# Two attention blocks on one core: residual copies replaced by additions that read x and x1 themselves

## The chip, the cores and the metric

The kernel runs on one core of a Trainium2 chip. A core has TensorE (PE, matrix products into PSUM; PEld is its weight load), VectorE (DVE), ScalarE (ACT), GpSimd (POOL) and SyncE (SP, which here issues every DMA). The engines run on their own and meet only at semaphores. The metric is the device time of one execution in microseconds, the median of several runs. Lower is better.

## The reference

Eight images of 256 channels and 32 x 32 pixels pass two attention blocks in a row, all in float32:

```
x : (8, 256, 1024)                       # image, channel, pixel
# layer 0
q = Wq x + bq ; k = Wk x + bk            # 32 channels each
v = Wv x + bv                            # 256 channels
x1 = gamma * (v softmax(q^T k)^T) + x
# layer 1
h  = group_norm(x1, 32 groups of 8 channels) * norm_w + norm_b
q, k, v = 256-channel projections of h, with biases
y  = x1 + proj( v softmax(q^T k / 16)^T ) + proj_b
```

Each layer therefore ends in a residual: layer 0 adds x, layer 1 adds x1. Since the rows of a softmax sum to one, the bias bv of layer 0 comes out as the constant gamma*bv per channel, and the output bias proj_b is a constant per channel too.

## The kernel before, in words

An image lies in SBUF as 128 partitions x 2 channel tiles (`CT`) x 1024 pixels. Products are made in near-float32 accuracy from pairs of a high and a low part (`_hi`, `_lo`), three matmuls for each product (`three`, lines 553 to 556). So every tensor that enters a product is split: mostly ACT writes the high part and DVE the low part.

The order of the work is written out by hand as a list of `Step`s (lines 78 to 199), and PE, ACT and DVE each walk through the same list. In the steady part one image takes a turn of 16 steps (`turn(i)`): the first 8 steps make the layer 0 attention tiles of image i (`keys`), the last 8 make the layer 1 attention tiles of image i - 1 (`logits`). The values product of a tile (`values`) follows its probabilities by two steps. So the layer 1 output of image i - 2 is complete in step 1 of turn i, and the layer 0 output of image i in step 9. PSUM is a ring of four slots of 128 x 1024: slots 0 and 1 mostly hold score tiles and projections, slots 2 and 3 hold the four banks of the running values product (`pv_ps`).

What the change touches:

- `evacuate` on DVE (lines 1050 to 1061) takes the four finished banks out of PSUM, 128 x 512 each. For layer 0 it writes x1 = gamma * bank + x1, in place (line 1057), for layer 1 res1 = bank + res1, in place (line 1060). What it adds was put into those buffers beforehand.
- That is done on POOL: `residual0` (line 461) writes x1 = 1 * x + gamma*bv from `x_in`, and `residual1` (line 453) writes res1 = 1 * x1 + proj_b. `unit` is a column of ones. POOL handles these in the order coefficients of the group norm, `hidden` (h in float32, line 439), `residual1`, `residual0` of the next image, four low parts of the layer 1 values (`split_value1`, line 468).
- SP issues the loads of x (line 390) and the stores of y (line 395) in one fixed row: after the store of image i comes the load of image i + 4. A load waits until `residual0` has copied the old content of its buffer, counted by `res0_ready`.
- `statistics` on DVE (lines 1063 to 1070) takes mean and variance of x1 per channel with two bn_stats for each half and two bn_aggr. PE averages them over the groups (`group_sums`, line 643, first the means, then variance plus squared distance of means), and `norm` on DVE (lines 1037 to 1048) makes what POOL needs for scale and offset.
- After step 1's evacuation, DVE goes on in its own order to low parts of the probabilities (`pt_lo`, line 1024), the low part of h (`h_lo`, line 919) and the second half of q and k of the next image (lines 977, 978, 985). PE needs these for the first `scores` tile of image i + 1 (line 564).

`link` makes DVE wait for its own preceding instruction, by a semaphore.

## Time and profile before

| | |
|---|---|
| median of 3 runs | 804.33 us (803.9 to 804.9) |
| the profiled execution's own time | 804.08 us |
| its span in the trace | 802.3 us |
| PE busy | 783.3 us (98%) |
| PEld busy | 646.1 us (81%) |
| DVE busy | 550.9 us (69%) |
| ACT busy | 469.2 us (58%) |
| POOL busy | 161.0 us (20%) |
| bytes read and written in HBM | 9.97 MB and 8.39 MB, 23 GB/s over the span |

The granted clock of TensorE was 0.995 of full speed over the span. The profiled execution's time lies 1.8 us above its span. The engines' busy times overlap, so none of them adds to the time by itself: what counts is where PE stands still and for whom.

### The profile page before, as it was taken

The numbers are of one execution on the slowest core, as the hardware profiler recorded it, in microseconds if no ns is written. First come the engines' busy times: TensorE is split into PE (matmuls) and PEld (weight loads), VectorE is DVE, ScalarE is ACT, GpSimd is POOL, SyncE is SP. The second block draws the span as 40 slices with busy tenths as digits, with TensorE's granted clock in tenths as the row PEclk, the third lists the DMA queues.
The fourth block names the chain that finished last, engine by engine and source line by source line (L and its number), as shares of the span: only waits on it lengthen the run. The fifth ranks groups of instructions, "written<-read, shape, count | busy, mean of one in ns | idle before, by whom it ended". The sixth has DMA issues, their size and how long they took to land.

```text
span 802.3 us, 9810 instructions
## 1 busy us (share of the span) xinstructions
PE 783.3 (98%) x3816; PEld 646.1 (81%) x3816; DVE 550.9 (69%) x790; ACT 469.2 (58%) x605; POOL 161.0 (20%) x144
## 2 busy tenths in 40 slices
PE   8899989999999999999999999999999999999998
PEld 8687868887888878888788877888788888887886
DVE  5866858778578765787657785676856765575564
ACT  4886556568455775567655586456855565444342
POOL 4800142023100241004210141102310024103300
PEclk9999999999999999999999999999999999999999
DMA  6100010002000110001100011000100010000101
GB/s 184 52 1 1 1 52 1 1 2 105 1 1 1 48 58 1 1 1 53 54 1 1 1 52 53 2 1 0 53 1 1 0 46 8 1 0 1 53 1 52
DMA packets 10365, 18.98 MB, mean 24 GB/s; under 512 B 2128, under 2 KB 3920, under 8 KB 10320
## 3 DMA queue, kind: packets, MB, share of 16 engines
q1 hardware_dynamic: 10320, 18.36, 6.6%
q8 instruction: 30, 0.49, 0.3%
q14 instruction: 15, 0.12, 0.0%
HBM read 9.97 MB, written 8.39 MB: 23 GB/s over the span
## 4 chain that ended last, share of the span: by engine, by line
PE 82%; DVE 11%; ACT 5%; issue 2%; ACTq 0%; POOL 0%; DVEq 0%; POOLq 0%
PE ring L554 25%; PE ring L556 24%; PE ring L555 24%; PE ring L564 4%; PE ring L574 3%; DVE h_lo L919 2%; DVE pt_lo L1024 2%; DVE res L1060 2%; DVE q L985 1%; PE ring L551 1%; ACT prob L773 1%; ACT prob L776 1%; DVE neg_raw L1009 1%; DVE k L977 1%; ACT pt_hi L787 1%
## 5 line engine op out<-in xcount | busy, mean ns | idle before, releaser
L554 PE MATMUL ring<-pt_hi,v_hi 128*128 128x512 f32 x512 | 202.8, 396 | 0.6 <-DVE pt_lo L1027 0.6
L556 PE MATMUL ring<-pt_hi,v_lo 128*128 128x512 f32 x512 | 201.2, 393 | 0.0
L555 PE MATMUL ring<-pt_lo,v_hi 128*128 128x512 f32 x512 | 201.1, 393 | 0.0
L776 ACT ACTIVATE prob<-ring,neg_max 128x1024 f32<-128x1024 f32 x64 | 71.6, 1118 | 160.2 <-DVE neg_max L1010 160.2
L468 POOL TENSOR_TENSOR v_lo<-v_f,v_hi 128x512 fp32r<-128x512 f32 x32 | 43.2, 1351 | 424.7 <-ACT v_hi L814 424.7
L1009 DVE TENSOR_REDUCE neg_raw<-ring 128x1 f32<-128x1024 f32 x64 | 78.3, 1223 | 71.6 <-PE ring L556 71.5
L554 PEld LDWEIGHTS ring<-pt_hi,v_hi 128*128 128x128 f32 x512 | 96.7, 189 | 21.8 <-issue 1.6
L556 PEld LDWEIGHTS ring<-pt_hi,v_lo 128*128 128x128 f32 x512 | 96.6, 189 | 21.3
L555 PEld LDWEIGHTS ring<-pt_lo,v_hi 128*128 128x128 f32 x512 | 96.9, 189 | 19.0
L1024 DVE TENSOR_TENSOR pt_lo<-prob,pt_hi 128x1024 fp32r<-128x1024 f32 x64 | 80.5, 1258 | 35.7 <-ACT pt_hi L787 35.5
L1007 DVE TENSOR_REDUCE neg_max<-ring 128x1 f32<-128x1024 f32 x64 | 77.8, 1222 | 33.7 <-PE ring L564 33.5
L554 PE MATMUL ring<-h_hi,query_hi 128*128 128x512 f32 x256 | 100.4, 392 | 0.0
L555 PE MATMUL ring<-h_lo,query_hi 128*128 128x512 f32 x256 | 99.9, 390 | 0.0
L556 PE MATMUL ring<-h_hi,query_lo 128*128 128x512 f32 x256 | 99.9, 390 | 0.0
L797 ACT ACTIVATE ring<-ring,neg_max 128x1024 f32<-128x1024 f32 x64 | 69.5, 1085 | 45.4 <-DVE neg_max L1007 45.0
L1027 DVE SCALAR_TENSOR_TENSOR pt_lo<-prob,row_inv,pt_hi 128x1024 fp32r<-128x1024 f32 x64 | 83.7, 1307 | 12.0 <-ACT pt_hi L790 12.0
L773 ACT ACTIVATE prob<-ring 128x1024 f32<-128x1024 f32 x64 | 65.4, 1021 | 33.6 <-PE ring L574 33.5
L790 ACT ACTIVATE pt_hi<-prob,row_inv 128x1024 fp32r<-128x1024 f32 x64 | 73.7, 1152 | 9.7 <-DVE row_inv L1016 9.6
L787 ACT CAST pt_hi<-prob 128x1024 fp32r<-128x1024 f32 x64 | 67.3, 1051 | 5.3
L556 PEld LDWEIGHTS ring<-h_hi,query_lo 128*128 128x128 f32 x256 | 48.1, 188 | 10.2
L554 PEld LDWEIGHTS ring<-h_hi,query_hi 128*128 128x128 f32 x256 | 48.1, 188 | 10.0 <-DVE v_lo L965 0.2
L555 PEld LDWEIGHTS ring<-h_lo,query_hi 128*128 128x128 f32 x256 | 48.1, 188 | 9.6
(135 smaller groups left out, 1225.5 us busy)
## 6 DMA issues: line engine op xcount, KB each, us to landing
out_y<-res SPq DMA_DIRECT2D x32, 256.0 KB, 2.2
x_in<-in_x SPq DMA_DIRECT2D x7, 1024.0 KB, 4.8
x_in<-in_x SPq DMA_DIRECT2D x2, 512.0 KB, 5.0
h_f<-in_wv_t SPq DMA_DIRECT2D x1, 256.0 KB, 4.4
res<-in_wq SPq DMA_DIRECT2D x1, 256.0 KB, 7.1
res<-in_wk SPq DMA_DIRECT2D x1, 256.0 KB, 7.3
res<-in_wv SPq DMA_DIRECT2D x1, 256.0 KB, 7.6
res<-in_wp_t SPq DMA_DIRECT2D x1, 256.0 KB, 7.7
```

Of the source, the lines that this page charges most:

```text
L554: mm(out, w_hi, m_hi, start=first, stop=False)
L555: mm(out, w_hi, m_lo, start=False, stop=False)
L556: return mm(out, w_lo, m_hi, start=False, stop=last)
L773: activation(prob[:, p % PROBS], ring[:, slot], ACT.Exp).then_inc(S["keys_exp"], 1)
L776: activation(prob[:, p % PROBS], ring[:, slot], ACT.Exp, bias=neg_max[:, k % 2:k % 2 + 1], accum_out=row_sum[:, k % 2:k % 2 + 1]).then_inc ...
L787: copy(pt_hi[p % PT][:], prob[:, p % PROBS]).then_inc(S["p_hi"], 1)
L790: activation(pt_hi[p % PT][:], prob[:, p % PROBS], ACT.Identity, scale=row_inv[:, k % 2:k % 2 + 1]).then_inc(S["p_hi"], 1)
L797: activation(ring[:, slot], ring[:, slot], ACT.Exp, bias=neg_max0[:, k:k + 1], accum_out=row_sum0[:, k:k + 1]).then_inc(S["scores_exp"], 1)
L1007: V.tensor_reduce(neg_max0[:, k:k + 1], src, AX_X, ALU.max, negate=True).then_inc(S["scores_max"], 1)
L1009: link(V.tensor_reduce(neg_raw[:, k % 2:k % 2 + 1], src, AX_X, ALU.max, negate=True))
L1024: V.tensor_tensor(lo[:], src, hi[:].bitcast(F32), ALU.subtract).then_inc(S["p_split"], 1)
L1027: V.scalar_tensor_tensor(lo[:], src, row_inv[:, k % 2:k % 2 + 1], hi[:].bitcast(F32), ALU.mult, ALU.subtract).then_inc(S["p_split"], 1)
```

## The change

`residual0` and `residual1` are gone from POOL, with `unit` and `res1`. There are now two buffers x1, used in turn by even and odd images, in the room of x1 and res1. The layer 0 evacuation reads x from `x_in` and writes gamma * bank + x to x1, so what stands there now is smaller than the true x1 by gamma*bv in each channel. The layer 1 evacuation adds its bank, x1 and a column `gbv_bp` = gamma*bv + proj_b in one instruction, in place in x1, and the stores of y read x1. The group norm is corrected by the same constant: one DVE instruction more after the two bn_aggr adds gamma*bv to the channel means, and the mean that goes into the offset of h has it subtracted (this takes the place of a copy).

The four layer 1 weight matrices, which were loaded into res1 at the start, are loaded into x1[1] now. For image 0 POOL copies x once into x1[0] (`keep_first_x`), so that image 2 can be loaded early. Every later load waits until the layer 0 evacuation has read its buffer (`pv_read`), and a layer 0 evacuation from image 2 on waits for the stores of two images before.

```diff
--- before.py
+++ after.py
...
@@ -274,11 +274,10 @@
 
         x_in = [sb(f"x_in{j}", [P, CT, N]) for j in range(2)]
         x_hi, x_lo = pair("x", [P, CT, N])
-        x1 = sb("x1", [P, CT, N])
+        x1 = [sb(f"x1_{j}", [P, CT, N]) for j in range(2)]
         h_f = sb("h_f", [P, CT, N])
         v1_f = sb("v1_f", [P, 2, 2, C])
         h_hi, h_lo = pair("h", [P, CT, N])
-        res1 = sb("res1", [P, CT, N])
         query_hi, query_lo = pair("query", [P, CT, N])
         v0_hi, v0_lo = pair("v0", [P, TILES, C])
         v1_hi, v1_lo = pair("v1", [P, TILES, C])
...
@@ -386,13 +384,16 @@
                     sp.dma_start(dst, src).then_inc(S[ready], 16)
 
             def load(i):
-                sp.wait_ge(S["res0_ready"], i - 1)
+                if i == 2:
+                    sp.wait_ge(S["x0_kept"], 1)
+                else:
+                    sp.wait_ge(S["pv_read"], PHASE_NO[0, i - 2] * BANKS + BANKS)
                 sp.dma_start(x_in[i % 2][:], x_v[i]).then_inc(x_loaded[i % 2], 16)
 
             def store(i):
                 for b, (half, ct) in enumerate(bank_of):
                     sp.wait_ge(S["pv_read"], PHASE_NO[1, i] * BANKS + b + 1)
-                    sp.dma_start(y_v[i][:, ct, half_cols[half]], res1[:, ct, half_cols[half]]).then_inc(S["y_stored"], 16)
+                    sp.dma_start(y_v[i][:, ct, half_cols[half]], x1[i % 2][:, ct, half_cols[half]]).then_inc(S["y_stored"], 16)
 
             sp.wait_ge(S["x_split"], 2)
             load(2)
...
@@ -445,22 +446,15 @@
                 pool.wait_ge(S["h_hi"], CT * i + 1)
                 G.tensor_tensor(h_lo[:, 0], h_f[:, 0], h_hi[:, 0].bitcast(F32), ALU.subtract).then_inc(S["h_split"], 1)
 
-            def residual1(i):
-                pool.wait_ge(S["bias_read"], 1)
-                if i > 0:
-                    pool.wait_ge(S["y_stored"], 16 * BANKS * i)
-                for ct in range(CT):
-                    last = G.tensor_scalar(res1[:, ct], x1[:, ct], unit[:], bp_s[:, ct:ct + 1], ALU.mult, ALU.add)
-                last.then_inc(S["res1_ready"], 1)
-
-            def residual0(i):
-                if i > 0:
-                    pool.wait_ge(S["res1_ready"], i)
-                    pool.wait_ge(S["h_hi"], CT * i)
-                for ct in range(CT):
-                    last = G.tensor_scalar(x1[:, ct], x_in[i % 2][:, ct], unit[:], gbv[:, ct:ct + 1],
-                                           ALU.mult, ALU.add)
-                last.then_inc(S["res0_ready"], 1)
+            def keep_first_x():
+
+                pool.wait_ge(S["x0_loaded"], 16)
+                pool.wait_ge(x_loaded[0], x_loads(0))
+                G.tensor_copy(x1[0][:], x_in[0][:]).then_inc(S["x0_kept"], 1)
+
+            def bias_sums():
+
+                G.tensor_tensor(gbv_bp[:], gbv[:], bp_s[:], ALU.add).then_inc(S["sums_ready"], 1)
 
             def split_value1(i, m):
                 pool.wait_ge(S["v1_hi"], 4 * i + m + 1)
@@ -502,16 +496,14 @@
 
             G.memset(ones[:], 1.0).then_inc(S["ones_ready"], 1)
             G.memset(neg_half[:], -0.5).then_inc(S["ones_ready"], 1)
-            G.memset(unit[:], 1.0).then_inc(S["ones_ready"], 1)
-            pool.wait_ge(S["ones_ready"], 3)
+            pool.wait_ge(S["ones_ready"], 2)
             small_things()
             first_values0()
             first_split_x()
             pool.wait_ge(S["shift_ready"], 1)
             bias_rows()
-            pool.wait_ge(S["x0_loaded"], 16)
-            pool.wait_ge(x_loaded[0], x_loads(0))
-            residual0(0)
+            bias_sums()
+            keep_first_x()
             split_weights()
             pool.wait_ge(x_loaded[0], x_loads(2))
             pool.wait_ge(S["ring_ready"], RING_NO["value0", 0, 3] + 1)
@@ -525,9 +517,6 @@
                 hidden(i)
                 if i in H_LO_HALVES:
                     split_hidden(i)
-                residual1(i)
-                if i + 1 < IMAGES:
-                    residual0(i + 1)
                 for m in range(4):
                     split_value1(i, m)
 
...
@@ -1039,7 +1028,7 @@
                 dve.wait_ge(S["ring_ready"], RING_NO[entry] + 1)
                 got = norm_place(entry)
                 if m == 0:
-                    V.tensor_copy(group_mean[:], got)
+                    V.tensor_tensor(group_mean[:], got, gbv[:], ALU.subtract)
                     link(V.tensor_tensor(dev[:], mean_var[:, :, 0], got, ALU.subtract))
                     link(V.tensor_tensor(dev2[:], dev[:], dev[:], ALU.mult))
                     last = V.tensor_tensor(spread[:], dev2[:], mean_var[:, :, 1], ALU.add)
@@ -1049,25 +1038,31 @@
 
             def evacuate(layer, i):
                 first = PHASE_NO[layer, i] * BANKS
-                dve.wait_ge(S[("res0_ready", "res1_ready")[layer]], i + 1)
+                if layer == 0 and i == 0:
+                    dve.wait_ge(S["x0_kept"], 1)
+                    dve.wait_ge(S["sums_ready"], 1)
+                if layer == 0 and i >= 2:
+                    dve.wait_ge(S["y_stored"], 16 * BANKS * (i - 1))
+                x_from, x_to = x_in[i % 2] if i else x1[0], x1[i % 2]
                 for b, (half, ct) in enumerate(bank_of):
                     cols = half_cols[half]
                     dve.wait_ge(S["pv_ready"], first + b + 1)
                     if layer == 0:
-                        V.scalar_tensor_tensor(x1[:, ct, cols], pv_ps[:, b], gamma_s[:], x1[:, ct, cols],
+                        V.scalar_tensor_tensor(x_to[:, ct, cols], pv_ps[:, b], gamma_s[:], x_from[:, ct, cols],
                                                ALU.mult, ALU.add).then_inc(S["pv_read"], 1)
                     else:
-                        V.tensor_tensor(res1[:, ct, cols], pv_ps[:, b], res1[:, ct, cols],
-                                        ALU.add).then_inc(S["pv_read"], 1)
+                        V.scalar_tensor_tensor(x_to[:, ct, cols], pv_ps[:, b], gbv_bp[:, ct:ct + 1], x_to[:, ct, cols],
+                                               ALU.add, ALU.add).then_inc(S["pv_read"], 1)
 
             def statistics(i, half):
                 dve.wait_ge(S["pv_read"], PHASE_NO[0, i] * BANKS + BANKS)
                 for ct in range(CT):
-                    last = V.bn_stats(bn[:, ct, half * 6:(half + 1) * 6], x1[:, ct, half_cols[half]])
+                    last = V.bn_stats(bn[:, ct, half * 6:(half + 1) * 6], x1[i % 2][:, ct, half_cols[half]])
                 if half == HALVES - 1:
                     link(last)
                     V.bn_aggr(mean_var[:, 0], bn[:, 0])
-                    V.bn_aggr(mean_var[:, 1], bn[:, 1]).then_inc(S["stats_ready"], 1)
+                    link(V.bn_aggr(mean_var[:, 1], bn[:, 1]))
+                    V.tensor_tensor(mean_var[:, :, 0], mean_var[:, :, 0], gbv[:], ALU.add).then_inc(S["stats_ready"], 1)
 
             def follow(entry):
                 if entry[0] == "keys":
```

The order of instructions on DVE is the same but for one more in `statistics` and another kind of instruction in two places. First, DVE from the last layer 1 tiles of turn 2 into turn 3 (step 1's evacuation with what follows it). Before:

```order
L985 SCALAR_TENSOR_TENSOR q_0<-ring,bqk_s,q_0 32x512
L1060 TENSOR_TENSOR res<-ring,res 128x512 x4
L1024 TENSOR_TENSOR pt_lo<-prob,pt_hi 128x1024
L919 TENSOR_TENSOR h_lo<-h_f,h_hi 128x1024 x2
L1024 TENSOR_TENSOR pt_lo<-prob,pt_hi 128x1024
L977 TENSOR_SCALAR k_0<-ring,bqk_s 32x512
L978 SCALAR_TENSOR_TENSOR k_0<-ring,bk_s,k_0 32x512
L985 SCALAR_TENSOR_TENSOR q_0<-ring,bqk_s,q_0 32x512
```

The same place in the changed kernel:

```order
L974 SCALAR_TENSOR_TENSOR q_0<-ring,bqk_s,q_0 32x512
L1054 SCALAR_TENSOR_TENSOR x_1<-ring,gbv_bp,x_1 128x512 x4
L1013 TENSOR_TENSOR pt_lo<-prob,pt_hi 128x1024
L908 TENSOR_TENSOR h_lo<-h_f,h_hi 128x1024 x2
L1013 TENSOR_TENSOR pt_lo<-prob,pt_hi 128x1024
L966 TENSOR_SCALAR k_0<-ring,bqk_s 32x512
L967 SCALAR_TENSOR_TENSOR k_0<-ring,bk_s,k_0 32x512
L974 SCALAR_TENSOR_TENSOR q_0<-ring,bqk_s,q_0 32x512
```

Nothing moved here; the four evacuations became scalar_tensor_tensor, with three operands instead of two. Second, DVE at the end of step 12 of turn 2, from the statistics to the means of the groups. Before:

```order
L1066 BN_STATS bn<-x 128x6 x2
L1069 BN_AGGR mean_var<-bn 128x2
L1070 BN_AGGR mean_var<-bn 128x2
L1009 TENSOR_REDUCE neg_raw<-ring 128x1
L1010 TENSOR_SCALAR neg_max<-neg_raw,row_const 128x1
L1027 SCALAR_TENSOR_TENSOR pt_lo<-prob,row_inv,pt_hi 128x1024
L1016 RECIPROCAL row_inv<-row_sum 128x1
L1042 COPY group_mean<-ring 128x2
L1043 TENSOR_TENSOR dev<-mean_var,ring 128x2
```

After:

```order
L1060 BN_STATS bn<-x_0 128x6 x2
L1063 BN_AGGR mean_var<-bn 128x2
L1064 BN_AGGR mean_var<-bn 128x2
L1065 TENSOR_TENSOR mean_var<-mean_var,gbv 128x2
L998 TENSOR_REDUCE neg_raw<-ring 128x1
L999 TENSOR_SCALAR neg_max<-neg_raw,row_const 128x1
L1016 SCALAR_TENSOR_TENSOR pt_lo<-prob,row_inv,pt_hi 128x1024
L1005 RECIPROCAL row_inv<-row_sum 128x1
L1031 TENSOR_TENSOR group_mean<-ring,gbv 128x2
L1032 TENSOR_TENSOR dev<-mean_var,ring 128x2
```

One small addition now stands between the statistics and the row maximum of the next tile. Third, POOL through one image. Before:

```order
L431 TENSOR_TENSOR norm_c<-nb_s,norm_t 128x2
L439 TENSOR_SCALAR h_f<-x,norm_a,norm_c 128x1024 x2
L453 TENSOR_SCALAR res<-x,unit,bp_s 128x1024 x2
L461 TENSOR_SCALAR x<-x_in,unit,gbv 128x1024 x2
L468 TENSOR_TENSOR v_lo<-v_f,v_hi 128x512 x4
L428 TENSOR_TENSOR rstd<-var_eps,neg_half 128x2
```

After:

```order
L432 TENSOR_TENSOR norm_c<-nb_s,norm_t 128x2
L440 TENSOR_SCALAR h_f<-x_0,norm_a,norm_c 128x1024 x2
L462 TENSOR_TENSOR v_lo<-v_f,v_hi 128x512 x4
L429 TENSOR_TENSOR rstd<-var_eps,neg_half 128x2
```

Four large POOL instructions per image are gone and nothing came in their place.

## Rows read from the trace of the kernel before

**Rows 1.** The page's engine row: busy us, share of the span, instructions.

```profile
PE 783.3 (98%) x3816; PEld 646.1 (81%) x3816; DVE 550.9 (69%) x790; ACT 469.2 (58%) x605; POOL 161.0 (20%) x144
```

**Rows 2.** Busy time by stretch of the span: one steady turn of 96 us.

```profile
282.00:378.00 96.00, 95.53 (x466) 78.67 (x465) 68.58 (x99) 58.90 (x78) 17.58 (x15) 1.00 0.06 23
```

**Rows 3.** Waits of PE: who waited for whom, us in total, times, longest.

```profile
PE ring L564 <- DVE q L985: 3.3, 6, 0.7
```

**Rows 4.** Timeline of PE at scores' first tile: start us, us, what [idle before].

```profile
190.40 0.70 PE L564 MATMUL ring<-k,q 96*128 96x512 f32 x2 [0.72 <-DVE q L985]
286.30 0.70 PE L564 MATMUL ring<-k,q 96*128 96x512 f32 x2 [0.46 <-DVE q L985]
```

**Rows 5.** Timeline of DVE from step 1's evacuation of turn 3 on.

```profile
276.71 2.48 DVE L1060 TENSOR_TENSOR res<-ring,res 128x512 f32<-128x512 f32 x4
279.11 1.22 DVE L1024 TENSOR_TENSOR pt_lo<-prob,pt_hi 128x1024 fp32r<-128x1024 f32 x1
280.24 2.35 DVE L919 TENSOR_TENSOR h_lo<-h_f,h_hi 128x1024 fp32r<-128x1024 f32 x2
282.51 1.22 DVE L1024 TENSOR_TENSOR pt_lo<-prob,pt_hi 128x1024 fp32r<-128x1024 f32 x1
...
285.30 0.74 DVE L985 SCALAR_TENSOR_TENSOR q<-ring,bqk_s,q 32x512 fp32r<-32x512 f32 x1
```

**Rows 6.** Groups by line, the two evacuations: busy us, mean ns, idle before.

```profile
L1057 DVE SCALAR_TENSOR_TENSOR x<-ring,gamma_s,x 128x512 f32<-128x512 f32 x32 | 21.8, 742 | 0.0
L1060 DVE TENSOR_TENSOR res<-ring,res 128x512 f32<-128x512 f32 x32 | 20.0, 683 | 1.3 <-PE ring L556 1.1
```

**Rows 7.** Timeline of DVE, layer 0 evacuation in turn 2.

```profile
230.19 2.72 DVE L1057 SCALAR_TENSOR_TENSOR x<-ring,gamma_s,x 128x512 f32<-128x512 f32 x4
```

**Rows 8.** Timeline of DVE at the end of the program.

```profile
797.06 2.67 DVE L1060 TENSOR_TENSOR res<-ring,res 128x512 f32<-128x512 f32 x4 [1.12 <-PE ring L556]
```

**Rows 9.** Timeline of DVE around the statistics and norm of turn 3.

```profile
347.72 0.15 DVE L1070 BATCH_NORM_AGGREGATE mean_var<-bn 128x2 f32<-128x12 f32 x1
347.88 1.23 DVE L1009 TENSOR_REDUCE neg_raw<-ring 128x1 f32<-128x1024 f32 x1
...
351.07 0.16 DVE L1044 TENSOR_TENSOR dev<-dev 128x2 f32<-128x2 f32 x1
351.26 0.16 DVE L1045 TENSOR_TENSOR spread<-dev,mean_var 128x2 f32<-128x2 f32 x1
351.34 0.68 DVE L965 TENSOR_TENSOR v_lo<-ring,v_hi 128x512 fp32r<-128x512 f32 x1
```

**Rows 10.** Timeline of PE at the group sums of turn 3 and of image 7.

```profile
352.07 0.28 PE L643 MATMUL ring<-spread,group_s 128*128 128x2 f32 x2
722.55 0.35 PE L643 MATMUL ring<-spread,group_s 128*128 128x2 f32 x2 [0.76 <-DVE spread L1045]
```

**Rows 11.** Timeline of POOL: residual copies at the start, in turn 2 and turn 3.

```profile
31.51 2.39 POOL L461 TENSOR_SCALAR x<-x_in,unit,gbv 128x1024 f32<-128x1024 f32 x2
190.07 3.44 POOL L461 TENSOR_SCALAR x<-x_in,unit,gbv 128x1024 f32<-128x1024 f32 x2
282.37 3.54 POOL L453 TENSOR_SCALAR res<-x,unit,bp_s 128x1024 f32<-128x1024 f32 x2 [11.14 <-DMA out_y<-res]
```

**Rows 12.** Timeline of DVE in turn 2, turn 7 and turn 8.

```profile
192.46 2.13 DVE L1024 TENSOR_TENSOR pt_lo<-prob,pt_hi 128x1024 fp32r<-128x1024 f32 x1
665.59 1.43 DVE L1024 TENSOR_TENSOR pt_lo<-prob,pt_hi 128x1024 fp32r<-128x1024 f32 x1 [0.64 <-ACT pt_hi L787]
746.09 1.28 DVE L960 SCALAR_TENSOR_TENSOR query_lo<-ring,query_b,query_hi 128x1024 fp32r<-128x1024 f32 x1 [1.98 <-ACT query_hi L817]
```

**Rows 13.** Timeline of SP: the load of image 4.

```profile
193.54 0.39 SPq L390 DMA_DIRECT2D x_in<-in_x  x1
```

**Rows 14.** DMA issues by line: count, KB each, median us to landing.

```profile
x_in<-in_x SPq DMA_DIRECT2D x7, 1024.0 KB, 4.8
```

**Rows 15.** Timeline of ACT: high part of x of image 4.

```profile
256.28 1.99 ACT L758 CAST x_hi<-x_in 128x1024 fp32r<-128x1024 f32 x2
```

More of the change, by code:

```diff
@@ L260 @@
     "v1_full", "v1_hi", "value1_split", "stats_ready", "norm_read", "coef_ready", "h_full", "h_hi", "h_split",
-    "x_hi", "x_split", "res0_ready", "res1_ready", "weights_read", "weights_split", "rows_ready", "bias_read",
+    "x_hi", "x_split", "x0_kept", "sums_ready", "weights_read", "weights_split", "rows_ready", "bias_read",
     "layer0_split", "v0_weights", "small_ready", "ones_ready", "key_hi", "link", "pool_link",
@@ L311, in build @@
         neg_half = sb("neg_half", [P, CT])
-        unit = sb("unit", [P, 1])
-        wq_f, wk_f, wv_f, wp_f = (res1[:, j // 2, (j % 2) * HALF:(j % 2 + 1) * HALF]
+        wq_f, wk_f, wv_f, wp_f = (x1[1][:, j // 2, (j % 2) * HALF:(j % 2 + 1) * HALF]
                                   .rearrange("p (t c) -> p t c", t=CT) for j in range(4))
@@ L326, in build @@
         bq_s, bk_s, bv_s, bp_s = (sb(f"{n}_s", [P, CT]) for n in ("bq", "bk", "bv", "bp"))
-        gbv = sb("gbv", [P, CT])
+        gbv, gbv_bp = sb("gbv", [P, CT]), sb("gbv_bp", [P, CT])
         query_b = sb("query_b", [P, CT])
@@ L438, in hidden @@
                 for ct in range(CT):
-                    G.tensor_scalar(h_f[:, ct], x1[:, ct], norm_a[:, ct:ct + 1], norm_c[:, ct:ct + 1],
+                    G.tensor_scalar(h_f[:, ct], x1[i % 2][:, ct], norm_a[:, ct:ct + 1], norm_c[:, ct:ct + 1],
                                     ALU.mult, ALU.add).then_inc(S["h_full"], 1)
@@ L762, in hidden @@
                 for ct in range(CT):
-                    activation(h_hi[:, ct], x1[:, ct], ACT.Identity, bias=norm_c[:, ct:ct + 1],
+                    activation(h_hi[:, ct], x1[i % 2][:, ct], ACT.Identity, bias=norm_c[:, ct:ct + 1],
                                scale=norm_a[:, ct:ct + 1]).then_inc(S["h_hi"], 1)
```

## The prediction

> **What bounds the kernel now.** I read the page's engine line first: PE is busy for 783.3 of 802.3 us [rows 1]. So at most 19 us can be won from anything that is not PE's own work, and the change leaves PE's instructions alone. The view by stretches says where those 19 us lie: a steady turn of 96 us has PE busy for 95.53 of it [rows 2], so the steady turns give back under 0.5 us each, and the rest of the idle time lies at the start, in the first two images and in the last. Then the waits of PE: the largest entry is the scores product waiting for the low part of q, 3.3 us in six waits [rows 3]. The timeline shows what they are: 0.72 us in turn 2, 0.46 us in turn 3 [rows 4], and turns 4, 5 and 6 repeat turn 3 to the hundredth. (0.72 + 4 x 0.46 = 2.56; the sixth, 0.74 us, is in the opening.) Turn 7 has no next image to score, so it has none.
>
> Last I followed DVE back from that wait. In turn 3 it runs without a gap from the layer 1 evacuation at 276.71 through pt_lo, h_lo, pt_lo and k to q, which ends at 285.30 + 0.74 = 286.04; PE starts at 286.30 [rows 4, 5]. The reader is to see there that each instruction starts where the one ahead lets it, none with an idle time in brackets. So whatever the evacuation gains or loses arrives at PE whole, once in each of five turns. This is the one place in the steady part where the change touches the path.
>
> **The change, part by part.**
>
> *The layer 1 evacuation.* It becomes the three-operand form that layer 0's evacuation already has: one bank from PSUM, one column, one tensor from SBUF, 128 x 512. The mean is 742 ns for that form and 683 ns for the present one, at the same size [rows 6]. What counts in a row of four is the time from start to start. Four of the present kind take 2.48 us, the last of it 0.68, so they start (2.48 - 0.68) / 3 = 0.60 us apart [rows 5, 6]. Four of the other take 2.72, the last 0.74: 0.66 us apart [rows 6, 7]. The price is 4 x 0.06 = 0.24 us for an evacuation. Where DVE is the path, in turns 2 to 6, it lengthens PE's wait: 5 x 0.24 = 1.20 us. After the wait PE and DVE are both later by the same amount, so nothing further comes of it within the turn. In turn 7 DVE has 0.64 us idle a little later, and in turn 8 it has 1.98 us idle after the evacuation [rows 12]: nothing there. At the end the four banks come 0.68 us apart, the pace of three matmuls (2.67 us for four [rows 8], less 0.68, over three is 0.66), and the new form keeps that pace, so only the last one's extra length shows: 0.06 us. Sum: +1.26 us.
>
> The two ends for this term: if the column in the add form costs nothing, it is 0; if the full length, not the spacing, were added and the end paid it four times over, it is 6 x 4 x 0.06 = 1.44. I take 1.26, since the form itself is in the trace 32 times, at 742 ns.
>
> *The addition to the statistics.* The trace has no such instruction at that place, so I bound it. Linked small operations start 0.19 us apart (351.07, 351.26), and the next instruction that needs nothing starts 0.08 behind (351.34) [rows 9]. Now the row maximum starts 0.16 behind the last bn_aggr (347.72, 347.88). With one linked addition between them this becomes 0.19 + 0.08 to 0.19 + 0.16, so DVE is later by 0.11 to 0.19 us, and 0.36 at most if two whole links came on top; below 0 it can't be, as nothing is taken away. The copy of the group means that becomes a subtraction is under 0.05 us either way. Is it covered? The row maximum behind it has no idle time ahead, so the delay travels along DVE to the spread, which ends at 351.42. PE takes the spread at 352.07 [rows 10], 0.65 us after. From q's end to PE's start it was 0.26 [rows 4, 5], so 0.4 us are free. I take 0, covered by PE's own values matmuls; the upper end, 0.36 with 0.05 for the subtraction, is just at the edge. In image 7 PE waits there already, 0.76 us [rows 10], and could wait 0.2 longer at most.
>
> *POOL without the copies.* Fifteen pairs of tensor_scalar go, 2.4 to 3.5 us each where the rows show them [rows 11], some 50 us of POOL. No wait of PE ends on them: DVE's evacuations never waited for them [rows 6], and the layer 1 values parts that follow on POOL wait for ACT anyway. The copies did slow DVE in places: pt_lo took 2.13 us at 192.46 while a copy ran from 190.07 to 193.51 [rows 11, 12], against 1.22 in rows 5, and 1.43 at 665.59. Both have slack behind them: at 192.46 no PE wait follows, at 665.59 there was idle time ahead. In the five stretches that are the path there is nothing to win: pt_lo at 282.51 ran beside the copy at 282.37 and took its usual 1.22 us [rows 5, 11]; it was the copy that stretched, to 3.54 us for what took 2.39 alone. I take 0, the ends are 0 and -2.56 - 1.2 us (all five waits gone, and the 1.20 that the evacuation adds to them).
>
> *The copy for image 0.* It stands where the first `residual0` stood, 2.39 us from 31.51, followed by nothing that PE waits for before image 2: 0.
>
> *Loads.* A load was released by the copy: image 4's at 193.54 [rows 13]. Now the layer 0 evacuation of image 2 releases it, which ends at 230.19 + 2.72 = 232.9 [rows 7]. It lands 4.8 us later [rows 14], at about 238, and ACT wants it at 256.28 [rows 15]: 18 us early. The row of SP is unchanged: behind a load stands the store of the next image, half a turn further on, so the longer waits hold up nothing. The evacuation's new wait for stores looks back at stores that were issued some 50 us before. All 0.
>
> *Sum.* 804.08 us (span 802.3 and 1.8 around it) + 1.26 = 805.34. The profiled execution lies 0.25 us under the median of 804.33, which with 1.26 would give 805.59. I say **805.5 us**, 0.15% slower in name. What a measurement of this kernel can tell from no change is about 0.2%, 1.6 us, so this forecast is mostly "the same": 802.7 to 805.9 counts as that.
>
> **The rivals.**
>
> *A. The freed port makes it faster.* DVE and POOL hinder each other, as the 2.13 us show. If copies cost the path more than I read, for example by small delays that hide in each instruction, DVE's chain of 9.3 us from 276.71 to 286.04 shortens. If it shortens by 0.7 us or more, wait and added cost both vanish: 804.08 - 2.56 + 0.06 = 801.6. Half as much gives 803. Against it: every instruction in rows 5 has its usual length, copy or no copy. Once 0.46 + 0.24 us are won per turn, more brings nothing.
>
> Here a rule speaks against my reading. The Trainium skill, "SBUF — State Buffer", section "SBUF: two separate sides", says that VectorE with two SBUF inputs and GpSimd share a port pair as an exclusive lock, held for the whole instruction, and that "the other fully blocks". By it pt_lo at 282.51 should have stood until the copy's first half was done, and taking copies away should win this at each such place. The rows of turn 3 don't agree (the copy stretched instead, 3.54 us), the one at 192.46 does in part (0.9 us of delay), and by the rule the time would be that of A.
>
> *B. The new form costs nothing here,* or PE's wait is partly the model of its matmul ends: 804.2.
>
> *C. The statistics leak, and it is slower.* The place is step 12, the mechanism a late spread: if the addition with its link and the subtraction make the spread later by more than 0.4 us, or ACT, which takes the row maximum there, pushes its row of casts behind it onto PE, then PE waits at the group sums in turns 2 to 7, for which nothing waited before. It decides at 0.4 us in turn 3. A leak of 0.2 to 0.4 us in six turns adds 1.2 to 2.4 to the forecast: 806.7 to 807.9. For it speaks that no idle time stands between statistics and maximum; against it the small size of every such operation.
>
> **How the numbers follow.** Forecast 0.64, with its own range of 804.8 to 806.3; A 0.08; B 0.15; C 0.13. Of the forecast's 0.64 some three tenths lie over 805.9. Slower by over 0.2%: 0.19 + 0.13 = 0.32. Faster by over 0.2%: A, of which a small part stays within: 0.07. The rest, 0.61, is the same. The range leaves out A and the upper part of C: 804.0 to 806.9.
>
> **What would show it.** Right: the layer 1 evacuation at 740 ns and 2.72 us for four; PE's wait for q at 0.70 us in turns 3 to 6 and 0.96 in turn 2; turns 96.15 us long where they were 95.9; x loads issued near 233 us with no ACT wait for them; POOL some 50 us less busy. Wrong: a wait for q below 0.46 (A), at 0.46 with an evacuation at 2.48 (B), or a PE wait for the spread at the group sums before image 7 (C). A PE wait elsewhere that is not in the trace now would mean that some slack I took as free was not.

## The result and the profile after

The changed kernel takes 805.86 us in the median of 19 runs (805.11 to 807.84), the kernel before 804.61 us in 19 runs (803.9 to 805.18). The ratio is 1.0016 with a 95% interval of 1.0009 to 1.0022. So it is slower by about 1.3 us: the whole interval lies above 1, though the difference is under the 0.2% that the prediction had set as the bound of "the same". The profiled execution took 805.45 us, with a span of 803.7 us.

The page's engine line, and the window of the steady turn, as in [rows 1, 2]:

```profile
span 803.7 us, 9764 instructions
PE 783.5 (97%) x3816; PEld 646.3 (80%) x3816; DVE 551.2 (69%) x798; ACT 468.3 (58%) x605; POOL 103.0 (13%) x113
```

```profile
282.00:378.00 96.00, 95.24 (x465) 78.40 (x465) 68.61 (x100) 58.54 (x77) 9.11 (x10) 1.00 0.06 22
```

POOL lost 58 us of work, 161.0 to 103.0. PE's busy time is the same to 0.2 us. But in the window of 96 us PE is busy for 95.24 us where it was 95.53: it stands still for 0.29 us more. The view of waits names the place, the same entry as in [rows 3], 4.5 us now and 3.3 before:

```profile
PE ring L553 <- DVE q L974: 4.5, 6, 0.9
```

PE's timeline of the changed kernel, the rows that answer to [rows 4] and the second of [rows 10], with the first matmul near 96 us as a mark (columns: start, duration, line, operation, idle time before it and what released it):

```profile
95.92 0.35 PE L543 MATMUL ring<-wv_hi,x_hi 128*128 128x256 f32 x1 [0.37 <-DVE spread L1034]
...
190.69 0.70 PE L553 MATMUL ring<-k,q 96*128 96x512 f32 x2 [0.88 <-DVE q L974]
...
286.85 0.70 PE L553 MATMUL ring<-k,q 96*128 96x512 f32 x2 [0.73 <-DVE q L974]
...
383.00 0.70 PE L553 MATMUL ring<-k,q 96*128 96x512 f32 x2 [0.72 <-DVE q L974]
...
479.19 0.70 PE L553 MATMUL ring<-k,q 96*128 96x512 f32 x2 [0.74 <-DVE q L974]
...
575.30 0.70 PE L553 MATMUL ring<-k,q 96*128 96x512 f32 x2 [0.71 <-DVE q L974]
...
723.89 0.35 PE L632 MATMUL ring<-spread,group_s 128*128 128x2 f32 x2 [0.76 <-DVE spread L1034]
```

The five waits for q make 3.78 us, against 2.56 in the prediction's sum: +1.22 us. The wait before image 7 is still 0.76 us, and no new wait has appeared between the waits for q in turns 3 to 6, whose turns are 96.1 to 96.2 us long.

DVE in turn 3, as in [rows 5], and the layer 0 evacuation, as in [rows 7]:

```profile
230.47 2.71 DVE L1051 SCALAR_TENSOR_TENSOR x<-ring,gamma_s,x_in 128x512 f32<-128x512 f32 x4
...
277.01 2.72 DVE L1054 SCALAR_TENSOR_TENSOR x<-ring,gbv_bp,x 128x512 f32<-128x512 f32 x4
279.65 1.21 DVE L1013 TENSOR_TENSOR pt_lo<-prob,pt_hi 128x1024 fp32r<-128x1024 f32 x1
280.79 2.35 DVE L908 TENSOR_TENSOR h_lo<-h_f,h_hi 128x1024 fp32r<-128x1024 f32 x2
283.06 1.21 DVE L1013 TENSOR_TENSOR pt_lo<-prob,pt_hi 128x1024 fp32r<-128x1024 f32 x1
284.31 0.74 DVE L966 TENSOR_SCALAR k<-ring,bqk_s 32x512 fp32r<-32x512 f32 x1
285.09 0.75 DVE L967 SCALAR_TENSOR_TENSOR k<-ring,bk_s,k 32x512 fp32r<-32x512 f32 x1
285.85 0.74 DVE L974 SCALAR_TENSOR_TENSOR q<-ring,bqk_s,q 32x512 fp32r<-32x512 f32 x1
```

The evacuation takes 2.72 us for four banks where it took 2.48. Everything behind it has the length it had. From its start to q's end it is 285.85 + 0.74 - 277.01 = 9.58 us; before it was 9.33. DVE still has no idle time in this row, so the whole difference arrives at PE. The view of the evacuation's line says that all 32 have this length (ns: least, median, most; then first and last start):

```profile
L1054 DVE SCALAR_TENSOR_TENSOR x<-ring,gbv_bp,x x32: 732/742/752, 180.9 to 800.4; 128x512 f32<-128x512 f32 x32
```

DVE's statistics and norm in the same turn, as in [rows 9]; L1065 is the new addition:

```profile
348.25 0.15 DVE L1064 BATCH_NORM_AGGREGATE mean_var<-bn 128x2 f32<-128x12 f32 x1
348.44 0.16 DVE L1065 TENSOR_TENSOR mean_var<-mean_var,gbv 128x2 f32<-128x2 f32 x1
348.52 1.22 DVE L998 TENSOR_REDUCE neg_raw<-ring 128x1 f32<-128x1024 f32 x1
...
351.89 0.16 DVE L1034 TENSOR_TENSOR spread<-dev,mean_var 128x2 f32<-128x2 f32 x1
...
352.92 0.16 DVE L1036 TENSOR_SCALAR var_eps<-ring 128x2 f32<-128x2 f32 x1 [0.27 <-PE ring L632]
```

The row maximum starts 0.27 us behind the last bn_aggr, before 0.16. The addition costs DVE 0.11 us, and DVE gets it back at once: it waits 0.27 us for PE at `var_eps`, where it waited 0.36.

DVE at the places of [rows 8, 12]: the second pt_lo of turn 2 and the last evacuation:

```profile
192.74 1.22 DVE L1013 TENSOR_TENSOR pt_lo<-prob,pt_hi 128x1024 fp32r<-128x1024 f32 x1
...
798.39 2.80 DVE L1054 SCALAR_TENSOR_TENSOR x<-ring,gbv_bp,x 128x512 f32<-128x512 f32 x4 [1.05 <-PE ring L545]
```

And one row each of the engines that lost the copies or took over the loads: POOL's single copy, as in [rows 11], SP's load of image 4, as in [rows 13], and ACT's split of it, as in [rows 15]:

```profile
31.91 1.90 POOL L453 COPY x<-x_in 128x2048 f32<-128x2048 f32 x1
```

```profile
233.21 0.39 SPq L391 DMA_DIRECT2D x_in<-in_x  x1
```

```profile
256.61 1.99 ACT L747 CAST x_hi<-x_in 128x1024 fp32r<-128x1024 f32 x2
```

ACT has no idle time ahead of the split: the later load is early enough.

### The profile page after: what moved, and what is told of

It reads as the page before. It is cut to its first block, busy times and chain, and to the rows that moved or that the text cites. A ratio compares the mean times of both kernels' runs of the same rounds, so it can differ in the third digit from the quotient of the medians.

```text
span 803.7 us, 9764 instructions
## 1 busy us (share of the span) xinstructions
PE 783.5 (97%) x3816; PEld 646.3 (80%) x3816; DVE 551.2 (69%) x798; ACT 468.3 (58%) x605; POOL 103.0 (13%) x113
## 4 chain that ended last, share of the span: by engine, by line
PE 77%; DVE 13%; ACT 7%; issue 2%; ACTq 0%; POOL 0%; DVEq 0%; POOLq 0%
PE ring L543 23%; PE ring L544 23%; PE ring L545 23%; PE ring L553 4%; PE ring L563 2%; DVE pt_lo L1013 2%; DVE x L1054 2%; DVE h_lo L908 2%; DVE neg_raw L998 2%; ACT prob L765 2%; ACT prob L762 1%; ACT pt_hi L776 1%; DVE k L966 1%; DVE q L974 1%; DVE k L967 1%
## 5 line engine op out<-in xcount | busy, mean ns | idle before, releaser
L1013 DVE TENSOR_TENSOR pt_lo<-prob,pt_hi 128x1024 fp32r<-128x1024 f32 x64 | 78.3, 1223 | 35.6 <-ACT pt_hi L776 35.3
```

What stands on the lines that cost most here:

```text
L1013: V.tensor_tensor(lo[:], src, hi[:].bitcast(F32), ALU.subtract).then_inc(S["p_split"], 1)
```

## The experiments

Two things are read of each run: its time against the kernel before on the same chip, and in its trace the five waits of PE for q (turns 2 to 6). I also give "the rest": the span from the first layer 0 values matmul near 96 us (the first row of PE's timeline above) to the end. What lies ahead of that matmul differs between the profiled executions, by 1.5 us, and by 4 us in e5 (it starts at 95.75 to 97.28 us, in e5 at 99.73), for a reason told under e3. Before: 802.26 - 95.75 = 706.51 us. After: 803.67 - 95.92 = 707.75 us, so +1.24.

| run | median (range, runs), us | ratio to before, 95% | waits for q, turn 2 and turns 3 to 6 | rest, us |
|---|---|---|---|---|
| before | 804.61 | | 0.72, 0.46 each | 706.5 |
| after | 805.86 | 1.0009 to 1.0022 | 0.88, 0.71 to 0.74 | 707.8 |
| e1 two operands | 804.51 (803.93 to 805.19, 11) | 0.9985 to 1.0004 | 0.69, 0.47 to 0.48 | 706.4 |
| e2 before, column form | 805.68 (805.13 to 806.74, 11) | 1.0005 to 1.0023 | 0.86, 0.70 to 0.71 | 707.8 |
| e3 no mean correction | 806.26 (805.55 to 808.45, 9) | 1.0012 to 1.0031 | 0.86, 0.72 to 0.73 | 707.7 |
| e4 bank before scores | 802.28 (801.87 to 802.95, 6) | 0.9961 to 0.9984 | none | 704.4 |
| e5 constant in the values | 805.75 (804.63 to 808.02, 11) | 1.0003 to 1.0021 | 0.71, 0.49 each | 706.5 |
| e6 e4 and e5 | 803.04 (802.24 to 803.4, 9) | 0.9968 to 0.9988 | none | 704.0 |
| e7 before, bank first | 802.34 (801.82 to 804.42, 7) | 0.9963 to 0.9984 | none | 704.2 |
| e8 pad behind last addition | 807.45 (806.64 to 807.62, 7) | 1.0019 to 1.0041 | 1.11, 0.94 to 0.96 | 708.8 |
| e9 pad behind first addition | 806.22 (805.12 to 809.81, 12) | 1.0009 to 1.0035 | 0.87, 0.73 each | 707.6 |
| e10 before, immediate form | 804.59 (804.02 to 805.33, 10) | 0.9989 to 1.0008 | 0.68, 0.46 to 0.47 | 706.5 |
| e11 bank first and pad | 803.15 (802.78 to 803.58, 10) | 0.9969 to 0.9989 | 0.41, 0.26 each | 705.4 |

**e1: the change with the old form of the layer 1 evacuation.** It leaves the constant gamma*bv + proj_b out of the result.

```diff
-V.scalar_tensor_tensor(x_to[:, ct, cols], pv_ps[:, b], gbv_bp[:, ct:ct + 1], x_to[:, ct, cols],
-                       ALU.add, ALU.add)
+V.tensor_tensor(x_to[:, ct, cols], pv_ps[:, b], x_to[:, ct, cols], ALU.add)
```

> The changed kernel, with the layer 1 evacuation back in its two-operand form (bank + x1); left out is the constant gamma*bv + proj_b of each channel in y. The POOL copies stay gone. My theory (all of the loss is the third operand's 0.06 us for each evacuation, five times on the path): the wait for q back at 0.46 us in turns 3 to 6, time back by 1.26 us, so 804.6 us where the kernel before has 804.6. Rival (the freed POOL gives something that the evacuation hides): below the kernel before by 0.5 us or more. Rival (the loss comes from loads, from the statistics or from the new buffers): stays 1 us above the kernel before.

DVE and PE of e1, turn 3:

```profile
276.87 2.48 DVE L1054 TENSOR_TENSOR x<-ring,x 128x512 f32<-128x512 f32 x4
```

```profile
286.46 0.70 PE L553 MATMUL ring<-k,q 96*128 96x512 f32 x2 [0.48 <-DVE q L974]
```

The evacuation and the wait are those of before, and so is the time. With that operand taken away nothing of the loss is left, and the absent copies bring nothing: rival A is out, by which e1 should have been near 801.6.

**e2: the kernel before with that one edit.** The copies stay; the evacuation multiplies the bank by `unit`, a column of ones.

```diff
-V.tensor_tensor(res1[:, ct, cols], pv_ps[:, b], res1[:, ct, cols], ALU.add)
+V.scalar_tensor_tensor(res1[:, ct, cols], pv_ps[:, b], unit[:], res1[:, ct, cols],
+                       ALU.mult, ALU.add)
```

> The kernel before, with nothing changed but the layer 1 evacuation: bank * 1 + res1 with the column of ones, in place of bank + res1. POOL's copies, loads and statistics as before. My theory: four evacuations take 2.72 us in place of 2.48, the wait for q is 0.70 us in turns 3 to 6, time +1.26 us, 805.9. Rival (the loss lies in the other parts of the change): no more than 0.3 us.

```profile
277.12 2.73 DVE L1060 SCALAR_TENSOR_TENSOR res<-ring,unit,res 128x512 f32<-128x512 f32 x4
```

```profile
286.95 0.70 PE L564 MATMUL ring<-k,q 96*128 96x512 f32 x2 [0.70 <-DVE q L985]
```

DVE's and PE's rows of e2 in turn 3 are those of the changed kernel to 0.03 us in length and wait, and its rest is 707.8 us. e1 and e2 together: this edit by itself makes the whole loss, with or without the copies.

**e3: the change without the correction of the means.** The addition, its link and the subtraction are gone, so the mean that the group norm takes away is wrong by gamma*bv.

```diff
-link(V.bn_aggr(mean_var[:, 1], bn[:, 1]))
-V.tensor_tensor(mean_var[:, :, 0], mean_var[:, :, 0], gbv[:], ALU.add).then_inc(S["stats_ready"], 1)
+V.bn_aggr(mean_var[:, 1], bn[:, 1]).then_inc(S["stats_ready"], 1)
-V.tensor_tensor(group_mean[:], got, gbv[:], ALU.subtract)
+V.tensor_copy(group_mean[:], got)
```

> The changed kernel without the correction of the means: the addition behind the two bn_aggr with its link is gone, and the subtraction is a copy again. Left out is gamma*bv in the group norm's mean, its variance and offset. My theory (this is covered): same time as the changed kernel, 805.9 us, within 0.2, and the spread ends some 0.15 us earlier with nobody waiting for it. Rival (statistics leak): 0.15 us for each of six turns comes back, 805.0.

Waits and rest are those of the changed kernel to 0.03 us. The correction is fully covered, and rival C is out. Yet the median is 0.4 us higher than the changed kernel's, and the profiled span is 0.8 us longer (804.5). The stretches of the opening tell why. First e3's, then the changed kernel's (columns: window, its length, busy time and count of PE, PEld, DVE, ACT and POOL, granted clock of TensorE, DMA share, GB/s):

```profile
70.00:80.00 10.00, 10.00 (x66) 8.55 (x65) 6.29 (x17) 6.35 (x8) 0.00 (x0) 1.00 0.01 2
80.00:90.00 10.00, 10.00 (x45) 8.50 (x44) 7.91 (x12) 5.41 (x7) 0.00 (x0) 0.83 0.00 0
```

```profile
70.00:80.00 10.00, 10.00 (x68) 8.65 (x68) 5.60 (x13) 6.47 (x9) 0.00 (x0) 1.00 0.01 2
80.00:90.00 10.00, 10.00 (x51) 8.39 (x50) 9.30 (x18) 6.61 (x8) 0.00 (x0) 1.00 0.00 0
```

In e3 the granted clock is 0.83 in the second stretch: the engine ran for a third of it, from about 80 to 83 us, at the lower of its two levels, 1.2 GHz, and the trace has 45 matmuls there in place of 51. Every profiled execution here has such time between 34 and 44 us, where PE stands idle twice in the opening; some have this second piece, which begins at 78 to 81 us, others not. In the same stretch e5 has 0.67, and e6 to e9 have 0.83. It comes in kernels with and without the change and isn't the edit's. What brings it on is not shown: PE was busy for all of the 10 us ahead of it. This is why the rest is compared, and why the two medians of e3 and the changed kernel, 0.4 us apart, are no finding.

The mean granted clock of every execution was measured too, not only the profiled one's, and it says the same: at 0.994 or less seven of e3's nine executions have a median of 806.37 us and nine of the changed kernel's nineteen one of 806.24; at 0.998 two of e3's took 805.55 and 806.13, five of the changed kernel's 805.61 to 805.90.

**e4: the wait for q taken away by a place.** In step 4 of the turn PE's first layer 0 scores tile is put behind the first bank of values, which needs nothing from DVE at that time.

```diff
+first_scores = [entry for entry in now.early if entry[0] == "scores" and entry[2] == 0]
 for entry in now.early:
-    fill(entry)
+    if entry not in first_scores:
+        fill(entry)
 if now.values:
     values(now.values, range(now.banks_first))
+for entry in first_scores:
+    fill(entry)
```

> The changed kernel, with PE's order changed at one place in each turn: the first scores tile of the next image, for which PE waits for q, goes behind the first bank of the values product of the same step (0.69 us of matmuls) instead of ahead of it. My theory: the 0.71 to 0.88 us waits for q in turns 2 to 6 are filled with this work, 3.5 us in all come back, 802.4 us, below the kernel before. Rival (DVE and ACT are as late for what comes next, and the wait only moves): the wait for q gone, but new waits of the same sum within ten microseconds behind it, time within 0.5 us of the changed kernel's.

PE of e4 in turn 3, where the three matmuls of the bank now stand ahead of the scores:

```profile
285.41 0.39 PE L543 MATMUL ring<-pt_hi,v_hi 128*128 128x512 f32 x1
285.64 0.40 PE L544 MATMUL ring<-pt_lo,v_hi 128*128 128x512 f32 x1
285.87 0.40 PE L545 MATMUL ring<-pt_hi,v_lo 128*128 128x512 f32 x1
286.30 0.71 PE L553 MATMUL ring<-k,q 96*128 96x512 f32 x2
```

PE no longer waits by its own record, and the rest is 704.4, 3.4 us under the changed kernel. That is nearly the 3.78 us of waits. It isn't all of it, and the starts show why: the matmuls of the bank start 0.23 us apart, but the scores tile 0.43 us behind the last of them, so q still comes 0.1 to 0.2 us late in each turn. PE's record hides it, because the modelled end of a matmul (0.40 us after its start) covers it. At 802.28 us this kernel is faster than both, 0.28% under the kernel before with an interval of 0.16 to 0.39%.

**e7: the same reorder in the kernel before.** If the change costs only through that wait, it should cost almost nothing here.

> The kernel before, with PE's first scores tile behind the first bank of the values product, nothing else. My theory: its five waits (0.72 and four of 0.46, 2.56 us) are filled, 802.1 us; the changed kernel with the same reordering measured 802.3, so the whole loss of the change, 1.26 us, vanishes but for 0.06 when PE doesn't wait there. Rival (the change costs 1.2 us of something beside this wait): 801.0 us.

PE's weight load of that tile in e7, all that still waits for q, and PE's rows there:

```profile
286.88 0.30 PEld L564 LDWEIGHTS ring<-k,q 96*128 96x128 f32 x2 [0.17 <-DVE q L989]
```

```profile
286.75 0.40 PE L556 MATMUL ring<-pt_hi,v_lo 128*128 128x512 f32 x1
286.99 0.63 PE L564 MATMUL ring<-k,q 96*128 96x512 f32 x2
```

The rest is 704.2 against 704.4 in e4. Where PE hardly waits for q, the change costs 0.2 us and not 1.24. A part of that stands at q again: here the scores tile starts 0.24 us behind the bank, at the matmuls' own pace, in e4 0.43. In the medians, 802.34 and 802.28, no difference is left.

**e8 and e9: a dose at two places.** The changed kernel with one useless addition of 128 x 160 on DVE, behind each layer 1 evacuation (e8) or behind each layer 0 evacuation (e9). A memset of the pad's source at the start goes with it.

```diff
+if layer == 1:   # e9: layer == 0
+    V.tensor_tensor(pad_to[:], pad_from[:], pad_from[:], ALU.add)
```

> The changed kernel with one useless DVE addition of 128 x 160 in SBUF (some 0.22 us by its size, measured against the 0.16 us of two columns) behind every layer 1 evacuation. My theory: each such microsecond reaches PE in turns 2 to 6: waits of 0.94 us, time +1.1 us, 807.0. Rival (DVE has slack, and the measured loss has another source): no change, 805.9.

> The changed kernel with the same useless addition of 128 x 160 behind every layer 0 evacuation, half a turn away from the other place. My theory (PE doesn't wait for DVE there, idle time of DVE follows within 2 us): no change, 805.9 us. Rival (any DVE time costs PE): +1.1 to 1.8 us, as at the other place.

e8, DVE and PE in turn 3:

```profile
280.98 0.32 DVE L1059 TENSOR_TENSOR pad_to<-pad_from 128x160 f32<-128x160 f32 x1
```

```profile
288.41 0.70 PE L555 MATMUL ring<-k,q 96*128 96x512 f32 x2 [0.94 <-DVE q L976]
```

e9, DVE in turn 3, the pad and the row maximum that follows later:

```profile
330.34 0.31 DVE L1059 TENSOR_TENSOR pad_to<-pad_from 128x160 f32<-128x160 f32 x1
...
334.77 1.23 DVE L1000 TENSOR_REDUCE neg_raw<-ring 128x1 f32<-128x1024 f32 x1 [1.18 <-PE ring L547]
```

The same instruction costs 0.20 to 0.25 us a turn at PE in one place (waits of 0.94 to 0.96 us for 0.71 to 0.74, the rest +1.04) and nothing in the other: in e9 DVE waits 1.18 us for PE some 3 us after the pad, where it waits 1.41 in the changed kernel, so the 0.23 us are absorbed there, and the rest is 707.6. A quarter of a microsecond of DVE has no price of its own; its place gives it one. The median of e9 lies 0.4 us over the changed kernel's, again with a piece at the lower clock at 80 to 84 us in its profiled execution. Its three executions with a granted clock of 0.996 took 805.12 to 805.30 us, the changed kernel's five with that clock 805.11 to 805.53.

**e10: is it the form or the column?** e2 again, with the number 1.0 in place of the column.

```diff
-V.scalar_tensor_tensor(res1[:, ct, cols], pv_ps[:, b], unit[:], res1[:, ct, cols],
+V.scalar_tensor_tensor(res1[:, ct, cols], pv_ps[:, b], 1.0, res1[:, ct, cols],
```

> The kernel before with the layer 1 evacuation as bank * 1 + res1, the 1 written into the instruction and not read from a column. If reading the column costs the 0.06 us for each instruction: four take 2.48 us and the time is the kernel before's, 804.6. If the three-operand form does, as I think: 2.72 us, waits of 0.70 us, 805.8.

```profile
277.19 2.48 DVE L1060 SCALAR_TENSOR_TENSOR res<-ring,res 128x512 f32<-128x512 f32 x4
```

```profile
286.78 0.70 PE L564 MATMUL ring<-k,q 96*128 96x512 f32 x2 [0.46 <-DVE q L985]
```

Here my expectation was wrong. DVE's four banks take 2.48 us, as in the two-operand form, and PE's wait is 0.46 us, as before. The three-operand form costs nothing; the column does. Where the prediction prices "the form", it should say "the column operand". This constant differs from channel to channel, so it can't be written as an immediate.

**e5 and e6: the constant put where it costs no column.** In e5 the constant goes into layer 1's value bias on PE, in the opening, and the evacuation is the two-operand one; e6 adds the reorder of e4.

```diff
-mm(value_b_ps[:, 0:C], bv_rows[:, o], wp_f[:, o], start=o == 0, stop=o == CT - 1)
+mm(value_b_ps[:, 0:C], bv_rows[:, o], wp_f[:, o], start=o == 0, stop=False)
+for ct in range(CT):                # out_diag: gbv_bp on a diagonal
+    mm(value_b_ps[:, ct * P:(ct + 1) * P], ones[:], out_diag[:, ct], start=False, stop=ct == CT - 1)
```

> The changed kernel with the constant gamma*bv + proj_b put into the bias of the layer 1 values, once at the start (two POOL multiplications with the identity, two matmuls of 128 columns more in the bias products), which a softmax with rows that sum to one carries into y unchanged. The layer 1 evacuation has two operands again; nothing is left out of the result. My theory: as the run without the constant, waits for q of 0.47 us, time level with the kernel before, 804.6 us, and 0.2 more at most for the two matmuls. Rival (something else in the changed kernel costs too): 805 or more.

> The constant in the value bias, and PE's first scores tile behind the first bank. My theory (0.24 us of DVE count only where PE waits for that chain, and in the reordered kernel it doesn't): nothing beyond the reordering alone but 0.06 us at the end, 802.2 us. Rival (shorter evacuations are worth 0.24 us wherever DVE is this full): 801.1 us.

A sentence of mine in the expectation of e5 is mistaken, and with it one in the account of the reference at the top. Layer 1's softmax is normalised over one pixel index and the values are summed over the other, so the product there is "v softmax(q^T k / 16)", without the transpose. A constant in v therefore does not come out as that constant: e5 and e6 add it weighted by the sums over the softmax. Their times stand, since no instruction depends on the value, but they are not versions of this kernel. (For layer 0, where the same trick is used, the two indices agree.)

The waits of e5 are nearly those of before (0.49) and its rest is 706.5, so the steady part behaves as expected. The median missed my 804.6 by 1.15 us. The profiled execution, the slowest of the eleven, shows an opening that ran at the lower clock for longer (0.67 at 80 to 90 us). The two executions with a granted clock of 0.995 and more took 804.63 and 804.77 us, the nine with less 805.39 to 808.02. In e6 it is alike: I expected 802.2, the two executions at 0.998 took 802.24 and 802.28, the seven at 0.993 and 0.994 802.75 to 803.4. e6's rest of 704.0 is 0.4 under e4's, where I had expected 0.06: q comes earlier there, and e4 still loses a little to it in each turn. Nine executions of eleven and seven of nine at the lower clock are many beside ten of 23 of the kernel before on that chip. That the additional work in the opening of e5 and e6 brings it on was not tested and stays open.

**e11: how much room the reorder leaves.** e4 with the pad of e8.

> The changed kernel with PE's first scores tile behind the first bank, and the useless DVE addition of 128 x 160 (0.23 us from start to start) behind every layer 1 evacuation. By PE's wait of 0.71 to 0.88 us against 0.69 us of matmuls put ahead of it, the reordered kernel stands near the edge: if PE now reaches the tile just as q is ready, each 0.23 us is paid again, 802.3 + 1.1 = 803.4 us. If there is slack left behind the edge (no wait is seen there), up to the same size it costs nothing: 802.3. My theory, from the arithmetic: the waits come back at some 0.2 us each, 803.4; the rival is the free one, 802.3.

```profile
286.73 0.70 PE L555 MATMUL ring<-k,q 96*128 96x512 f32 x2 [0.26 <-DVE q L980]
```

PE waits again, 0.26 us in each of turns 3 to 6, after 0.23 us more on DVE. The reorder has moved PE's bank of 0.7 us ahead of the wait, no more, and in e4 that room was already used up, as the 0.43 us showed. So the next quarter of a microsecond on DVE before q costs nearly its full length: from one such scores tile to the next it is 0.15 to 0.24 us longer than in e4 (95.7 us for 95.5), and the rest grows by 1.0.

## Why the prediction was right

The forecast was 805.5 us (own range 804.8 to 806.3), measured 805.86. Step by step:

- *Evacuation, 4 x 0.06 = 0.24 us in each of five turns, 1.20 us.* Measured: 2.72 us for 2.48, the chain from evacuation to q 0.25 us longer, waits 3.78 for 2.56, so 1.22. e2 makes it alone, e1 takes it back. In turns 3 to 6 the waits grew by 0.25 to 0.28 us. Turn 2 was forecast at 0.96 and came out at 0.88: part was hidden there, and a few hundredths more in the other turns made up for it.
- *End, 0.06 us.* The last evacuation takes 2.80 us for 2.67, 0.13 more, but it starts 0.07 sooner behind PE (1.05 us for 1.12). From the mark near 96 us to the group sums before image 7 the trace is 1.17 us longer (723.89 - 95.92, against 722.55 - 95.75 [rows 10]), and over the rest 1.24, so the end is worth 0.07. (The prediction calls the pace of the last banks 0.68 us and works out 0.66 for it; nothing hangs on that.)
- *Statistics, 0.11 to 0.19 us on DVE, none on PE.* Measured 0.11, given back at `var_eps`; e3 changes nothing past the opening. Rival C needed 0.4 us and had a quarter of that.
- *POOL, nothing.* 58 us less work, where some 50 were forecast, and in e1, where only this and the statistics are left, 804.51 us. The pt_lo that had been held up, 2.13 us [rows 12], takes 1.22 us now, and nothing waits behind it. The 64 pt_lo instructions of layer 0 together are 2.2 us shorter (mean 1223 ns for 1258), and none of it lies in the five places that count.
- *The port rule.* By the Trainium skill, "SBUF — State Buffer", section "SBUF: two separate sides", of a VectorE instruction with two SBUF inputs and a GpSimd instruction that reads SBUF, the one that starts first has the shared port pair for its whole length, and "the other fully blocks". The prediction read the rows of turn 3 as speaking against that, and this reading was too quick. The copy recorded at 282.37 begins inside DVE's h_lo, which has two inputs from SBUF too and runs from 280.24 to 282.59 [rows 5, 11], and pt_lo follows without a gap. The copy's 3.54 us are 2.39 and 1.15 more, about the length of that pt_lo. So the rows fit the rule, with POOL as the one that stood still (POOL's records are rough, so this is a reading and not shown by a run). At 192.46 it was the other way round: pt_lo ended 1.08 us after the copy did (193.51), close to its own length of 1.22, as if it had stood until then. What failed rival A is therefore not the rule but the place: in the chains that PE waits for POOL lost and not DVE, and DVE's delay, 0.9 us at the most, fell where nothing came of it.
- *Copy for image 0 and loads, nothing.* The load of image 4 goes out at 233.21 (forecast near 233), and ACT doesn't wait for it.
- *Rival B, no cost.* Out: 742 ns for a bank and 0.73 us at PE. That PE's wait is only its modelled ends is out too: by the starts of PE's scores tiles, which are recorded, the turns are 96.1 to 96.2 us long for 95.9.

One thing was wrong under a right number. I took the 0.06 us a bank from layer 0's evacuation and put it down to the three-operand form. Two things distinguished that row from the present one, the form and the column, and e10 shows that it is the column. The sum held because the changed kernel has both; by the prediction's words e10 should have cost 1.2 us, and it cost nothing. In this the number was right by luck: the row that it was taken from happened to have the column too.

## What to carry to other kernels

Work taken from an engine that nobody waits for, POOL here with 58 us, was worth nothing; the 0.24 us an evacuation that was paid for it stood on the one chain that PE waited for, and came back five times. Before adding a column operand to an instruction, follow its engine from there to the next wait of the bound engine, and count idle time in between: e8 and e9 are the same instruction at 1.0 and at 0 us. And where such a wait stands in every turn, look first for something ready that the waiting engine can do ahead of it: one bank moved in PE's order gave 3.4 us, more than twice what the whole change cost.

## What the runs showed of the hardware

- A per-partition column as operand costs DVE 0.06 us for each 128 x 512 instruction from PSUM: 742 ns with it (change and e2), 680 ns with the immediate 1.0 (e10), in otherwise the same scalar_tensor_tensor; 2.72 against 2.48 us for four.
- The granted clock of TensorE falls to the lower of its two levels in the opening of every profiled execution, between 34 and 38 us, where PE stands idle twice (in the changed kernel 1.68 us up to 35.64 and 1.23 us up to 37.57). In some it falls once more at 78 to 81 us, in e3 behind 10 us in which PE was busy throughout. That second piece (0.83 over 10 us in e3) made the opening 0.8 us longer. So single executions and small medians differ by about as much as this change costs: of the kernel before, beside e1 to e4, thirteen executions with a granted clock of 0.994 or less had a median of 805.1 us, four at 0.995 and 0.996 one of 804.0, seven above 804.6. The span past the opening tells more than the whole time.
- DVE's 0.11 us for a linked small addition is less than its own duration of 0.16 us: the row maximum behind it starts 0.08 us after its start (348.44, 348.52).
- DVE and POOL held each other up where both read SBUF: a pair of copies of 2.39 us took 3.54 us beside a pt_lo that kept its 1.22, and a pt_lo that started 2.4 us after another pair took 2.13.
